# Four-layer graph network on one core: node table split in four pieces, first unit's loads issued inside the node stage, 65 columns in attention, side-by-side PSUM columns, bf16 row products

## The reference

```
edge_index = stack([src, dst])
x = layernorm(x + gin0(x));  gin:  agg = segment_sum(x[src], dst);  h = mlp(x + agg)        (block 0 with batch norm)
x = layernorm(x + gin1(x));  the same with a hidden width of 256
x = layernorm(x + mpnn(x)):
    h = x @ enc_W + enc_b
    3 layers:  m = relu([h[src], h[dst], edge_features] @ msg_W1 + b1) @ msg_W2 + b2
               h = gru(segment_sum(m, dst), h)
    relu(h @ ro_W1 + b) @ ro_W2 + b
x = layernorm(x + gat(x)):
    2 layers:  h = x @ W;  e = leaky_relu((h @ a_src)[src] + (h @ a_dst)[dst])
               w = exp(e - segment_max(e)[dst]);  out = segment_sum(w / (sum w)[dst] * h[src], dst) + b
```

## Time and profile before

| | |
|---|---|
| Median of 3 runs | 3050.55 us (3045.49 to 3051.57) |
| The profiled execution's own time | 3055.14 us |
| Its span, first to last instruction | 3053.3 us |
| Busy: PE / POOL / DVE / ACT | 2648.6 / 2167.6 / 1920.8 / 1495.5 us |
| Mean granted TensorE clock | 0.915 of full speed |

### The profile page before, as it was taken

One profiled execution on the slowest core, in us unless ns is written; L12 is line 12 of the kernel. 1 busy time (PEld: TensorE's weight loads), 2 busy tenths in 40 slices (PEclk: granted clock), 3 DMA queues, 4 the chain that ended last, 5 costly groups with the idle time before them and its releaser, 6 DMA issues.

```text
span 3053.3 us, 73788 instructions
## 1 busy us (share of the span) xinstructions
PE 2648.6 (87%) x28348; PEld 2440.5 (80%) x28348; DVE 1920.8 (63%) x6097; ACT 1495.5 (49%) x2632; POOL 2167.6 (71%) x2178
## 2 busy tenths in 40 slices
PE   7999768999689999579998599995799995699991
PEld 6999738999559999369998289994499995599991
DVE  5877644554346888558888658887535555355555
ACT  7777528888334444244443344442634444244443
POOL 6777647777657777577777677776577775777773
PEclk9999858999789999789999799997799997699995
DMA  5666818999438999359998389995178883577771
GB/s 170 218 210 202 213 44 268 359 360 310 148 104 275 304 301 303 109 173 300 304 305 259 81 273 302 304 302 160 26 265 255 254 251 122 150 254 255 254 232 42
DMA packets 321464, 688.67 MB, mean 226 GB/s; under 512 B 114939, under 2 KB 150245, under 8 KB 302708
## 3 DMA queue, kind: packets, MB, share of 16 engines
q1 hardware_dynamic: 227584, 537.99, 52.5%
q0 software_dynamic: 69344, 70.04, 11.2%
q10 hardware_dynamic: 24340, 78.40, 6.6%
HBM read 487.50 MB, written 198.70 MB: 225 GB/s over the span
## 4 chain that ended last, share of the span: by engine, by line
PE 66%; POOL 12%; issue 8%; DVE 6%; ACT 4%; DMA 2%; SPq 1%; DVEq 0%; POOLq 0%; ACTq 0%
PE ps L1721 59%; POOL ringG L778 10%; PE ps L1675 3%; POOL nodes L778 2%; DVE ringG L1185 2%; PE ps L1684 1%; DMA big<-kept 1%; ACT big L951 1%; DVE edge_side L1185 1%; ACT big L896 1%; PE ps L1632 1%; PE ps L1742 1%; DVE ringG L1288 1%; ACT ringG L916 0%; PE ps L1780 0%
## 5 line engine op out<-in xcount | busy, mean ns | idle before, releaser
L1721 PE MATMUL ps<-big 128*128 128x192 bf16 (+1 forms) x25275 | 2258.3, 247 | 0.0
L1721 PEld LDWEIGHTS ps<-big 128*128 128x128 fp8e4 (+1 forms) x25275 | 2134.5, 98 | 61.6 <-issue 12.7
L778 POOL DMA_INDIRECT ringG<-tab,src_i x1596 | 1567.0, 982 | 528.1 <-issue 463.9
L1185 DVE SCALAR_TENSOR_TENSOR ringG<-ringG,same 128x64 f32<-128x64 f32 x2075 | 587.0, 283 | 148.5 <-ACT ringG L905 86.2
L896 ACT ACTIVATE big<-src_hot,node_minus 128x1536 fp8e4<-128x1536 int16 x242 | 368.9, 1573 | 211.4 <-PE ps L1721 192.9
L896 ACT ACTIVATE big<-big,node_minus 128x1536 fp8e4<-128x1536 int16 x239 | 364.4, 1573 | 203.9 <-PE ps L1721 191.6
L1185 DVE SCALAR_TENSOR_TENSOR edge_side<-edge_side,same 128x64 f32<-128x64 f32 x1245 | 349.6, 281 | 17.1
L778 POOL DMA_INDIRECT ringG<-in_x,src_i x266 | 285.5, 1073 | 101.2 <-issue 83.5
L1288 DVE SCALAR_TENSOR_TENSOR ringG<-ringG,expo 128x65 f32<-128x65 f32 x830 | 239.1, 288 | 156.7 <-ACT ringG L916 80.3
L863 ACT COPY big<-ps 128x384 f32<-128x384 f32 (+1 forms) x450 | 208.5, 481 | 218.5 <-PE ps L1721 215.7
L1170 DVE TENSOR_TENSOR big<-big 128x768 f32<-128x768 f32 (+3 forms) x78 | 72.9, 935 | 336.3 <-ACT big L863 330.3
(11 more groups left out here) (265 smaller groups left out, 1753.3 us busy)
## 6 DMA issues: line engine op xcount, KB each, us to landing
big<-kept SPq DMA_DIRECT2D x117, 1152.0 KB
big<-kept SPq DMA_DIRECT2D x78, 960.0 KB
sums<-ringG SPq DMA_DIRECT2D x260, 256.0 KB
kept<-big ACTq DMA_DIRECT2D x91, 576.0 KB
edge_side<-q_at_start SPq DMA_DIRECT2D x156, 256.0 KB
big<-kept SPq DMA_DIRECT2D x26, 1344.0 KB
big<-kept SPq DMA_DIRECT2D x52, 576.0 KB
big<-kept SPq DMA_DIRECT2D x39, 768.0 KB
```

What stands on the lines that cost most here:

```text
L778: return pool.indirect_dma_start(out=out_ap, out_offset=None, in_=table, in_offset=bass.IndirectOffsetOnAxis(ap=index, axis=0))
L1185: return v.scalar_tensor_tensor(now, before if u == 0 else source[:, (u - 1) * D:u * D], same[:, c:c + 1], now, ALU.mult, ALU.add)
L1721: mm = pe.matmul(ps[:, b, 0:256 + n] if wide else ps[:, b, to:to + n], hot[t][0:rows, u * P:(u + 1) * P], opener[:, 0:256 + n] if wide els ...
```

## The change

Five things are changed.

1. `split_table` works piece by piece (7, 6, 6 and 6 node tiles) and raises `split_ready` after each; PE waits in the first unit for the piece that it is about to use.
2. SP issues the loads of a pass's first unit earlier: in passes 2 to 4 pieces 0 and 1 behind the fifth chunk's table writes and the other two, as before, behind the seventh's; in pass 5 piece 0 behind the fourth chunk's writes and the other three behind the sixth's; in pass 6 all four ahead of the first chunk's writes. New waits on `FILL(...)` keep them from overwriting what the node stage still reads, and the turned tables `gT0` and `gT1` move from `FM[0]` to `FM[4]`. Pass 1 keeps its order.
3. In passes 5 and 6 the hot fetch brings 65 of the 66 values; the last, always 1, is written by a memset for each unit (`fetched = min(width, W)`).
4. The second column of a bank lies right behind the first (at column 192 or 195 instead of 256), so the opener is 384 or 390 columns wide and ACT evicts one contiguous run.
5. The row products take bf16 operands: `spans` becomes the bf16 `marks`, the destinations are split in two bf16 parts, and each product is two matmuls of 417 columns.

```
+        self.fetched = min(width, W)
...
-        opener = sb("opener", [P, 256 + 3 * WG], BF16)
+        opener = sb("opener", [P, 6 * W], BF16)
...
                     sp.dma_start(chunk_of(tab[2 + l], c), chunk(pq, c)).then_inc(table_out, 16)
                     sp.dma_start(chunk_of(qtab[l], c), chunk(pq, c, 2 * D)[:, :, D:]).then_inc(qtable_out, 16)
-
-                if l == 0:
-                    for q in range(len(TILES)):
-                        sp.wait_ge(hot_kept[q], 16 * TRIPS * KEEPING)
+                    if c == NC - 3:
+                        sp.wait_ge(*FILL(f"agg{l - 1}" if l else "l1_w2b", NC - 1))
+                        for q in range(2):
+                            sp.wait_ge(hot_kept[q], 16 * TRIPS * KEEPING)
+                            feed_piece(2 + l, 0, q)
+
                 load_hot_edges(l, 0)
-                feed_unit(2 + l, 0)
+                for q in range(2, len(TILES)):
+                    sp.wait_ge(hot_kept[q], 16 * TRIPS * KEEPING)
+                    feed_piece(2 + l, 0, q)
...
             for l in range(2):
+                if l:
+                    feed_unit(5 + l, 0)
                 for c in range(NC):
                     sp.wait_ge(*done(f"gh{l}", c))
                     sp.dma_start(chunk_of(tab[5 + l], c), chunk(gN, c, WG)).then_inc(table_out, 16)
                     sp.dma_start(chunk_of(adtab[l], c), chunk(adN, c, 2)).then_inc(adtab_out, 16)
-                feed_unit(5 + l, 0)
+                    if l == 0 and c == NC - 4:
+                        sp.wait_ge(*FILL("agg2", NC - 1))
+                        feed_piece(5, 0, 0)
+                    if l == 0 and c == NC - 2:
+                        sp.wait_ge(*FILL("l2_back", NC - 1))
+                        for q in range(1, len(TILES)):
+                            feed_piece(5, 0, q)
...
             def split_table(k, table):
...
+                    for q, t in enumerate(TILES):
+                        t = slice(t.start, t.stop)
+                        ins = split_rows(split[:, t], rest[:, t], table[:, t], w)
+                        if way.mixes(q):
+                            link(ins)
+                            ins = mixed_weights(k)
+                        if q == 0:
+                            link(ins)
+                            ins = v.tensor_copy(opener[:, 0:3 * w], split[:, 0])
+                        ins.then_inc(split_ready, 1)
...
-                    link(v.tensor_tensor(to.rearrange("p j (h d) -> p j h d", d=w), both, lead, ALU.add))
+                    to = to.rearrange("p j (h d) -> p j h d", d=w)
+                    link(v.tensor_tensor(to[:, :, :, 0:got], both, lead, ALU.add))
+                    if got < w:
+                        link(v.memset(to[:, :, :, got:w], 1.0))
...
-            link(v.tensor_scalar(FM[1], FM[6], below[:, 1:2], None, ALU.is_gt))
-            v.tensor_tensor(spans[:], spans[:], FM[1], ALU.subtract).then_inc(rows_ready, 1)
+            link(v.tensor_scalar(upto, FM[6], below[:, 1:2], None, ALU.is_gt))
+            link(v.tensor_copy(dst_parts[:, 0], dst_f[:]))
+            link(v.tensor_tensor(dst_parts[:, 1], dst_f[:], dst_parts[:, 0], ALU.subtract))
+            v.tensor_tensor(marks, spans[:], upto, ALU.subtract).then_inc(rows_ready, 1)
...
-                split, n = split_of(way), 3 * way.width
+                split, n = split_of(way), 3 * way.fetched
+                if first:
+                    pe.wait_ge(split_ready, len(TILES) * k + q + 1)
...
-                            b, to = u // 2, u % 2 * 256
+                            b, to = u // 2, u % 2 * n
...
-                            mm = pe.matmul(ps[:, b, 0:256 + n] if wide else ps[:, b, to:to + n],
-                                           hot[t][0:rows, u * P:(u + 1) * P], opener[:, 0:256 + n] if wide else split[0:rows, t],
+                            mm = pe.matmul(ps[:, b, 0:2 * n] if wide else ps[:, b, to:to + n],
+                                           hot[t][0:rows, u * P:(u + 1) * P], opener[:, 0:2 * n] if wide else split[0:rows, t],
...
-                pe.matmul(ps[:, 6 + t % 2, 0:L + 1], spans[:, t * P:(t + 1) * P], dst_f[:], start=True, stop=True
-                          ).then_inc(rows_in, 1)
+                for x in range(2):
+                    mm = pe.matmul(ps[:, 6 + t % 2, 0:L + 1], marks[:, t * P:(t + 1) * P], dst_parts[:, x], start=(x == 0),
+                                   stop=(x == 1))
+                mm.then_inc(rows_in, 1)
```

More of the change, by code:

```diff
@@ L394, in split_of @@
         def split_of(way):
-            return FM[7].bitcast(BF16)[:, 0:NT * 3 * way.width].rearrange("p (t j) -> p t j", t=NT)
+            return FM[7].bitcast(BF16)[:, 0:NT * 3 * way.fetched].rearrange("p (t j) -> p t j", t=NT)
         def eighths(at, size):
@@ L495, in build @@
         pq = FM[6].rearrange("p (t d) -> p t d", t=NT)
+        upto, marks = (FM[1].bitcast(BF16)[:, x * NP:(x + 1) * NP] for x in range(2))
+        dst_at = (3 * KEPT + KEPT + 2 * (NT - 4 * KEPT)) * UMAX * P // 4
+        dst_parts = big[:, dst_at:dst_at + L + 1].bitcast(BF16).rearrange("p (x n) -> p x n", x=2)
         turned = FM[2][:, 0:3 * D]
@@ L859, in evict @@
                     act.wait_ge(table_out, 16 * NC * k)
+                size = 3 * way.fetched
                 for b in banks:
@@ L863, in evict @@
                     nc.scalar.copy(parts_of(way)[:, 2 * b:2 * b + n].rearrange("p u k d -> p u (k d)"),
-                                   ps[:, b, :].rearrange("p (u x) -> p u x", u=2)[:, 0:n, 0:3 * way.width]
+                                   ps[:, b, 0:2 * size].rearrange("p (u x) -> p u x", u=2)[:, 0:n]
                                    ).then_inc(evicted, 1)
@@ L1080, in _ @@
                     f"gexp{l}": node_weights, "l3_square": square("gmix1"),
[L1081 removed]
+                    "gT1": lambda c, n: drain(FM[4][0:D, n], bank(c), ACT.Relu, g_b0[:]), "gh1": attention_table})
             act.wait_ge(spread_ready, 1)
@@ L1114, in split_rows, with mixed_weights @@
                 return v.tensor_tensor(split[:, :, 2 * w:], rest, split[:, :, w:2 * w], ALU.subtract)
+            def mixed_weights(k):
+                return v.tensor_copy(split_of(PASSES[k])[64:MIXED, NT - 1].rearrange("p (y d) -> p y d", d=D),
+                                     w_e_parts[64:MIXED, :, (k - 2) * D:(k - 1) * D])
             def split_table(k, table):
-                way = PASSES[k]
-                w, split, rest = way.width, split_of(way), rest_of(way)
-                if k != 2:
-                    link(split_rows(split, rest, table, w))
-                if way.mixes(len(TILES) - 1):
-                    link(v.tensor_copy(split[64:MIXED, NT - 1].rearrange("p (y d) -> p y d", d=D),
-                                       w_e_parts[64:MIXED, :, (k - 2) * D:(k - 1) * D]))
-                v.tensor_copy(opener[:, 0:3 * w], split[:, 0]).then_inc(split_ready, 1)
-                v.wait_ge(split_ready, k + 1)
+                way, parts = PASSES[k], len(TILES)
+                w, split, rest = way.fetched, split_of(way), rest_of(way)
+                if k == 2:
+                    link(mixed_weights(k))
+                    v.tensor_copy(opener[:, 0:3 * w], split[:, 0]).then_inc(split_ready, parts)
+                else:
+                    for q, t in enumerate(TILES):
[8 more added lines that the diff above has]
+                        ins.then_inc(split_ready, 1)
+                v.wait_ge(split_ready, parts * (k + 1))
             def split_chunk(c):
```

22 lines of the change are left out of this document (10 added, 12 removed).

## The result

The changed kernel takes 3035.76 us (median of 5 runs, 3030.97 to 3040.3) beside 3051.57 us for the kernel before (5 runs, 3045.49 to 3051.99): ratio 0.995, 95% interval 0.994 to 0.9961. It is faster, by 16 us where some 53 were forecast, and the time lies above the range (2978 to 3024). The profiled execution took 3030.97 us (span 3029.1), 24.2 us less in span than the one before, so it flatters the change by 8 us against the medians.

What follows compares the result with a forecast made beforehand. The prediction took PE as the bound, with POOL's gathers capping how much earlier passes could end. Gains per pass summed to 53.4 us, from 3055.1 to 3001.7 for the profiled execution, median 2997, range 2978 to 3024.

Steps and rivals of the forecast that it cites:

- POOL's room: End of passes 3 to 6: unless POOL starts earlier, they end at most 7.0, 0.4, 13.4 and 10.8 us earlier.
- table writes behind the early loads: Start of passes 2 to 5: table writes queue behind 2.1 or 3.5 MB; POOL delayed 0 to 5 us, taken as 0.
- Rival C: Early loads delay POOL by 5 us in passes 2 to 5, giving 3009 us; chance 0.15.
- What would show it: Listed trace signs; against the forecast: POOL's first gather of pass 5 over 5 us after the last scatter.
- Column pace: PE's units: narrower columns save 0.17 us per message unit and 0.57 per attention unit, 2.0 and 6.8 us a pass.
- rival D: Attention matmuls of 195 columns at odd starts are slow, costing 45 us in each attention pass: 3097 us; chance 0.05.
- Starts: PE's first product comes earlier in passes 2 to 6, by 5.3, 4.9, 5.3, 7.7 and 9.7 us.
- Rival E: Starts of passes don't move, leaving only columns and row products: 3022 us; chance 0.06.
- Row products: Pass 0: two bf16 matmuls take 0.36 us instead of 0.73, and POOL waits less: 10.6 us gained.
- Rival A: PE alone sets the passes' ends; passes 4 and 6 gain 6.2 and 5.0 us more: 2986 us; chance 0.15.

Runs made afterwards that it cites:

- e1: Changed kernel with the hole between a bank's two columns put back in message passes 2 to 4 (openers of 448 columns): 3014.67 us.
- e4: Kernel before with the narrower columns alone (65 fetched in attention, a bank's columns side by side): 3051.49 us, ratio 0.9998.
- e6: Changed kernel with a bank's two columns 224 apart in message passes 2 to 4 (openers of 416 columns): 3019.27 us.
- e10: Changed kernel, narrow openers kept, with each unit's first opener issued twice in message passes 2 to 4: 3015.61 us.
- e11: Changed kernel with most of pass 5's first-unit loads behind the table writes and edge_side added by way of PSUM: 3007.79 us.
- e3: Changed kernel with pieces 1 to 3 of pass 5's first-unit loads issued behind the table writes: 3029.09 us.
- e9: Changed kernel with wide message openers, pass 5's loads of pieces 1 to 3 behind table writes, and attention table rows 196 columns apart instead of 195: 3011.66 us.
- e7: Kernel before with the new starts alone (table split in four pieces, first unit's loads early): 3022.58 us.
- e2: Changed kernel with the edge_side addition as scalar_tensor_tensor instead of tensor_tensor: 3038.18 us.

## Why the prediction was wrong

The direction was right and the size too large by 29 us in the profiled executions. Most single prices were right; one assumption under the whole sum and one zero were wrong, and the columns of attention were priced at twice what they give.

**The failed step: "POOL's room".** The prediction took POOL's sequence of gathers as a fixed length (the 7.0, 0.4, 13.4 and 10.8 us of room from the earlier trace rows) and moved it with its start. It knew that DVE's two-input instructions prolong POOL's work, and applied this only to the scatters of the node stage. The gathers' length depends on how DVE's groups fall between them, and that hangs on PE's pace. The narrower openers, priced at +2.0 us in each message pass, cost 12, 11 and 8 us of POOL instead. Passes 2 to 4 were forecast at +15.3 and gave -7.0: 22.3 of the 29.2 us. Shown from both sides by e1, e4, e6, e10, and its mechanism by e11. In pass 6 the gathers took 4.1 us more as well (253.3 to 257.4 us), which is more than the 2.3 missing there; 3.8 of it are gathers caught by DVE's additions for the unit's products. That is read from the traces, and no run tests it alone.

**The wrong zero: table writes behind the early loads.** Rival C, given 0.15, holds in pass 5, and its size was underrated: 11 us of delay to POOL's start, not 5. Pass 5 gave 5.9 of 14.5: its room of 19 less 11 leaves 8, and the gathers took 2.4 us more (255.3 to 257.7). In passes 2 to 4 and 6 there was no such wait: from the last group's take-up to POOL's first gather took 93.5 us in pass 2 (93.1 before) and 75.3, 74.4 and 74.0 in passes 3, 4 and 6 (78.6, 76.6, 76.6 before). There POOL went from its scatters into the gathers without a stop, as it did before: the writes had landed in time. That the scatters cover a late write there was not tested. "What would show it" had named this sign, and e3 confirmed it.

**Column pace.** Message passes: right. The unit fell by 0.16 us (0.17 forecast), a bank takes 1.23, as forecast. Attention: a bank takes 1.27 to 1.28 where 1.27 was forecast (2306.20 to 2307.47), but the unit fell by 0.26 and not 0.57, so twelve units are worth 3.1 us and not 6.8. It shows in e3, where POOL no longer holds pass 5 up: the pass gains 10.7 of the 14.5 us (441.7 us from take-up to take-up, 452.4 before). The reason given for rival D, odd row starts, was real and small: 0.21 us a unit (e9), some 0.7 ns a matmul, where D had 12.6. The last 0.1 us of the unit stays open.

**Starts.** Right in every pass, within 1.3 us. From the last group's take-up to PE's first product the changed kernel is shorter by 5.1, 5.1, 4.0, 7.4 and 10.8 us in passes 2 to 6; forecast were 5.3, 4.9, 5.3, 7.7 and 9.7. None waits for `big<-kept` any more; DVE's first piece comes last in passes 5 and 6 and ACT's first tile in pass 2, as argued (in passes 3 and 4 PE goes into its first product without a stop):

```profile
886.35 0.48 PE L1759 MATMUL ps<-opener,big 128*128 128x384 bf16 x1 [0.34 <-ACT big L913]
...
2200.87 0.48 PE L1759 MATMUL ps<-opener,big 128*128 128x390 bf16 x1 [3.60 <-DVE opener L1154]
...
2614.27 0.48 PE L1759 MATMUL ps<-opener,big 128*128 128x390 bf16 x1 [3.35 <-DVE opener L1154]
```

Rival E is out; e7 alone gave 28 us.

**Row products.** A pair begins at 156.41 and the next product at 156.77: 0.36 us, as forecast. POOL's wait at 335 us is gone and one of 4.53 us is left. Pass 0 gained 13.5 instead of 10.6; 4.6 us of shorter gathers (285.5 to 280.9) lie in it, which had not been counted.

**Rival A** (PE alone sets the ends) fell with the same rows as the forecast: POOL sets them in all five passes.

**Do the parts add up?** Alone, by medians: starts 28.0, row products 8.1, columns 1.2 (no difference that can be measured): 37 us, and together 15.8. The 21 us between are what the columns take away once the other parts have used up POOL's room. In the kernel before, such catches cost nothing as long as POOL has room: in e4 pass 2's last group is taken up 356.7 us after POOL's first gather, 356.9 before, although the gathers took 10 us more. With the columns wide again in message passes (e1) the other parts' gain is back: 38 us by the medians.

## What to carry to other kernels

When the slack between two engines is read from a trace, the second engine's length is no constant: ask which of its instructions are prolonged by the first one's, and whether the change moves the two against each other. A cut of 0.16 us in a 26 us unit cost 12 us a pass here, so measure a small pacing gain alone (e4) before it is put in with others. And a small write that someone waits for doesn't go behind megabytes in the same queue.

## What the runs showed of the hardware that was not expected

- A gather that starts within about the first 0.5 us of a 0.69 us VectorE addition with both inputs in SBUF ends 0.82 us after that addition's end, whenever it began (1.39 us long at 0.1, 1.14 at 0.4). Behind one of 0.36 us (e11) it is 0.82 us too. With one input in PSUM the gather takes 0.94 or 0.95 us.
- Such delays can fall into step with the pace of the other engines: DVE's groups and POOL's four gathers both take 5.26 us, the collision repeats, and POOL begins 19 gathers in a unit of 25.83 us where it began 20 in 25.99.
- The form (tensor_tensor or scalar_tensor_tensor) makes no difference (e2).
- One more matmul in each unit of passes 2 to 4 made the kernel 20 us faster (3035.8 to 3015.6).
- 195 bf16 columns that start at odd places cost 0.21 us in 300 matmuls (26.01 against 25.80 us a unit).
